# Memory attention of a two-layer perceiver: one weighting per pair laced with a memory unit's long products

## The chip, the cores and the metric

The kernel runs on one core of one Trainium2 chip. The metric is the device time of one execution in microseconds; several executions are timed and the median is taken. TensorE multiplies (the trace has its products as PE and its weight loads as PEld), VectorE is DVE, ScalarE is ACT, GpSimd is POOL, and SP issues most transfers.

## The reference, cut to what matters

Two layers of attention and feed-forward blocks work on x (32 batches of 32 tokens, 512 wide) with a context of 257 tokens per batch. The change lies in the cross attention of the second layer. The kernel's keys and values of a context token are one and the same projection (`mem`), joined to the projections of the 32 own tokens:

```python
q = split_heads(xn @ Wq)
k = split_heads(kv[..., :INNER]);  v = split_heads(kv[..., INNER:])
mem = split_heads(memories @ Wm)          # memories: 257 context tokens
k = concatenate([k, mem]);  v = concatenate([v, mem])
attn = softmax(q @ k.T * 64 ** -0.5)      # 16 heads of 64, 289 keys
out = (attn @ v) @ Wo + bo
```

## The kernel before, in words

The batches go in 16 pairs (`PAIRS`), and turn `pr` of one loop (line 1117 on, on TensorE) works on the attention of pair `pr` while it makes the memory projections of pair `pr + 1`.

**A memory unit** (`memory(pr, units)`, lines 962 to 974) is one of eight groups of 128 rows of `mem`, for both batches of a pair: twelve long products, 128 x 512 elements each, into one PSUM bank. Context and weights are split in a high and a low half so that three products of reduced precision stand for one: eight products of the context's high half (line 970; `cth`, with `wmh` and `wml` in turn over four slices k) and four of its low half (line 973, `ctl`). ScalarE makes the high half (`split_high`, line 1663) once all eight units of the pair before are done, VectorE then the low half (`split_low`, line 2407). Units 2, 3 and 4 (`BY_DVE`) use the four banks that VectorE empties, the others those of ScalarE. A bank is opened in a fixed order, and each opening waits until the one four before it was emptied.

**The weighting** (`weighted(bb)`, lines 1060 to 1089) is attention times values for one batch: three parts, block 0 and block 1 of 128 context tokens each and a tail of 33 tokens. A part is 16 small products in fp32 with a 32-column weight tile and 64 moving columns; the trace has two records for each, so 64 for the two blocks and 32 for the tail (line 1074). The three parts add up in one bank, whose filling is signalled after the tail. In the 14 middle pairs the values and probabilities come through transfers (line 2862 from `value_turn`, lines 2859 and 1752 from DRAM `probs`), which the weighting waits for.

**A turn on TensorE** (line 1117 on) issues in this order: the scores of the first batch b0 (line 1032); the weighting of the batch before, b0 - 1; units 2 and 3; the scores of b1; unit 4; units 0 and 1; the transposes of the output rows (line 1043), every fourth turn the output projection (line 1114); units 5 and 6; the tail transposes (`prob_tail`, line 1057); unit 7; the weighting of b0. Between tail transposes, then: unit 7, first weighting (b0), scores, second weighting (b0 - 1 of the next turn), units 2 and 3, scores, units 4, 0, 1, output rows, units 5, 6. `at_edge(pr)` is true for the first and the last turn, which turn their values and probabilities on TensorE instead.

**VectorE** in a turn, in program order: maxima of the first batch's scores (`maxima`, lines 2451 and 2453); the division and copy of the second weighting (`weighted`, line 2465); four 32 x 32 value transposes (`turn_values`, line 2426); copies of units 2 and 3 (line 2461); maxima of the second batch; transposes of its probabilities (line 2435); copy of unit 4; and so on to the tail copy (line 2520), `split_low`, the reciprocal (line 2528) and the division of the first weighting (line 2465 again). **ScalarE**: four exponentials for each batch as its maxima arrive (line 1689; each frees one of its banks, and the one unit 0 uses is among them), then the copies of units 0, 1, 5, 6, 7 and `split_high`. **SP**: the context of pair `pr + 2`, the next pair's own keys, value tails and queries (`load_pair`, which waits for the second weighting), the value moves, then two slices of a later stage's weights.

Of the kernel before, what the change touches and what calls it, by code (L numbers as in the profile page):

```python
# [92 lines left out]
def perceiver(nc, dram, out):  # L93
# [6 lines left out]
    with ctx:  # L100
# [3 lines left out]
        def sem(name):  # L104
            return ctx.enter_context(nc.semaphore(name))
# [5 lines left out]
        def tab(name, rows=128):  # L111
            a, n = TABLE_AT[name]
            return consts[0:rows, a:a + n]
# [49 lines left out]
        with ExitStack() as until_last:  # L163
            def shared_r(name, shape):
                return until_last.enter_context(nc.sbuf_tensor(name, shape, f32r))

            over(10240)
            ctl = shared_r("ctl", [128, 4, 2, 256])
            wmh = shared_r("wmh", [128, 2, 4, 512])
# [3 lines left out]
            wml = shared_r("wml", [128, 2, 4, 512])  # L173
# [3 lines left out]
            cth = shared_r("cth", [128, 4, 2, 256])  # L177
# [63 lines left out]
        dve_bank_full, dve_bank_free = sem("dve_bank_full"), sem("dve_bank_free")  # L241
# [113 lines left out]
        def W(name):  # L355
            return arena[:, slot_of[name], :, :]
# [40 lines left out]
        def at_edge(pr):  # L397
            return pr in (0, PAIRS - 1)
# [88 lines left out]
        def ch(c):  # L487
            return slice(512 * c, 512 * c + 512)
# [4 lines left out]
        def tl(t):  # L493
            return slice(128 * t, 128 * t + 128)
# [5 lines left out]
        def _(pe):  # L500
            stage = [0]
            mm = nc.tensor.matmul
# [7 lines left out]
            def open_act(key):  # L510
                u = UA.new(key)
                if u >= 4:
                    pe.wait_ge(act_bank_free, u - 3)
                return UA.banks[u % 4]

            def open_dve(key):
                u = UV.new(key)
                if u >= 4:
                    pe.wait_ge(dve_bank_free, u - 3)
                return UV.banks[u % 4]  # L520

            def on_act(key):
                pe.wait_ge(act_bank_free, UA.at[key] + 1)

            def on_dve(key):
                pe.wait_ge(dve_bank_free, UV.at[key] + 1)
# [57 lines left out]
            for t in range(TT):  # L584
# [4 lines left out]
                for i, (name, high, low) in enumerate((("qf", lq_high, lq_low), ("kf", lk_high, lk_low))):  # L589
                    pe.wait_ge(S["a_wlo"], i + 1)  # L590
                    b = open_dve((name, t)) if i else open_act((name, t))
# [15 lines left out]
            b = open_dve("corr")  # L607
# [7 lines left out]
            for c in range(C2):  # L615
                for k in range(4):
                    b = open_act(("agg", c, k))
                    for t in range(4 * c, 4 * c + 4):
                        last = mm(b[:, tl(t % 4)], VA[:, t, tl(k)], RA["mt"][:, t, :], start=True, stop=True)
                    last.then_inc(act_bank_full, 1)  # L620
            pe.wait_ge(S["a_wlo"], 4)
            for c in range(C2):
                on_act(("agg", c, 3))
                for o in range(4):
                    b = open_dve(("ao", o, c))
# [22 lines left out]
            for c in range(C2):  # L648
# [5 lines left out]
                b = open_act(("clock", c))  # L654
                for k in range(4):
                    last = mm(b[0:16, :], RB["cw"][:, k, :], XN[:, k, ch(c)], start=(k == 0), stop=(k == 3))
# [114 lines left out]
            for t in range(TT):  # L771
# [3 lines left out]
                b = open_act(("v", t))  # L775
                for k in range(4):
                    last = mm(b[:, :], XN[:, k, tl(t)], W("bv")[:, k, :], start=(k == 0), stop=(k == 3))
# [33 lines left out]
            for c in range(C2):  # L811
                for o in range(4):
                    b = open_dve(("bo", o, c))
                    for k in range(2 if c else 3, 4):
                        last = mm(b[:, :], W("bo")[:, k, tl(o)], RB["ot"][:, k, ch(c)], start=(k == (2 if c else 3)), stop=(k == 3))
# [44 lines left out]
            for j in range(NQ):  # L860
                for o, c in b1_order(j):
                    b = open_act(("b1", j, o, c))
# [14 lines left out]
            for c in range(C2):  # L877
# [3 lines left out]
                for k in range(4):  # L881
                    on_act(("feat", 2, c, k))
                    for i in range(4):
                        t = 4 * c + i
                        for n, (y_, w_) in enumerate(((y_high, sim_high), (y_low, sim_high), (y_high, sim_low))):
                            last = mm(four[i][:, :], y_[:, k, tl(t)], w_[:, k, :], start=(k == 0 and n == 0), stop=(k == 3 and n == 2))
                        if k == 3:
                            last.then_inc(act_bank_full, 1)
            for j in range(NQ):
                for o in range(4):  # L890
                    for c in range(C2):
                        b = open_act(("cg", j, o, c))
                        split_linear(b, ("cg", j), o, y_high, y_low, c).then_inc(act_bank_full, 1)
                        b = open_dve(("cu", j, o, c))
# [67 lines left out]
            def memory(pr, units):  # L962

                pe.wait_ge(S["d_chi"], pr + 1)
                for o in units:
# [7 lines left out]
                        last = mm(bank, wmh[:, o // 4, k, tl(o % 4)], ctl[:, k, :, :], start=False, stop=(k == 3))  # L973
                    last.then_inc(dve_bank_full if o in BY_DVE else act_bank_full, 1)

            def last_memory():

                on_act(("mrow", 1))
                b = open_act("m256")
                for o in range(OT1):  # L980
                    last = nc.tensor.transpose(b[:, 32 * o:32 * o + 32], last_rows[0:32, tl(o)], tab("ident", 32)[:, 0:32])
                last.then_inc(act_bank_full, 1)
# [32 lines left out]
            def value_blocks(bb):  # L1015

                for blk in range(2):
                    for half in range(2):
                        b = open_dve(("vt", bb, blk, half))
                        for o in range(4):  # L1020
                            last = nc.tensor.transpose(b[:, tl(o)], kts[bb // 2 % 2][:, 4 * half + o, bb % 2, 128 * blk:128 * blk + 128],
                                                       tab("ident"))
                        last.then_inc(dve_bank_full, 1)
# [33 lines left out]
                    last = nc.tensor.transpose(b[:, tl(g)], RDa["p"][:, g, 256:384], tab("ident"))  # L1057
                last.then_inc(dve_bank_full, 1)

            def weighted(bb):  # L1060

                i = bb % 2
                on_dve(("ptail", bb // 2))
                b = open_dve(("pv", bb))

                def part(lhs, rhs, first, row, stop):
                    for g in range(4):
                        for c in range(4):
                            o, par = 4 * (g // 2) + c, g % 2
                            if row is None:  # L1070
                                of = rhs[:, 2 * par:2 * par + 2, 32 * o:32 * o + 32]
                            else:
                                of = rhs[:, 128 * o + 64 * par:128 * o + 64 * par + 64].rearrange("p (a n) -> p a n", a=2)
                            last = mm(b[32 * c:32 * c + 32, 64 * g:64 * g + 64].rearrange("p (a n) -> p a n", a=2),  # L1074
                                      lhs(g, c), of,
                                      start=(first and g == 0), stop=stop, tile_position=(row or 0, 32 * c),
                                      skip_group_check=True)
                    return last

                if not at_edge(bb // 2):  # L1080
                    pe.wait_ge(values_full, 192 * (bb // 2))
                    pe.wait_ge(values_kept, 4 * (bb // 2))
                    pe.wait_ge(probs_full[i], 64 * (bb // 2))
                for blk in range(2):
                    part(lambda g, c: probs_moved[i][:, c, blk, 32 * g:32 * g + 32], RD["vt"][:, 2 * i + blk], blk == 0, None, False)
                if i == 0:
                    pe.wait_ge(tail_full[bb // 2 % 2], 32 * (bb // 4 + 1))
                part(lambda g, c: RDx["ptail"][64 * i:64 * i + 33, 0, 128 * g + 32 * c:128 * g + 32 * c + 32], RD["vtail"][64 * i:64 * i + 33, bb // 2 % 2], False, 64 * i, True
                     ).then_inc(dve_bank_full, 1)

            pe.wait_ge(S["d_wlo"], 1)
            memory(0, range(4))
# [5 lines left out]
            for h in range(2):  # L1098
                b = open_act(("mrow", h))
                for k in range(4):  # L1100
                    for i, (c_, w_) in enumerate(((last_high, wmh), (last_low, wmh), (last_high, wml))):
                        last = mm(b[0:32, :], c_[:, k, :], w_[:, h, k, :], start=(k == 0 and i == 0), stop=(k == 3 and i == 2))
# [14 lines left out]
            for pr in range(PAIRS):  # L1117
                b0, b1 = 2 * pr, 2 * pr + 1

                def fill(*units):  # L1120
                    if pr + 1 < PAIRS:
                        memory(pr + 1, [o for o in units if pr or o not in EARLY])

                on_dve(("mem", pr, 4))
                on_act(("mem", pr, OT1 - 1))
                pe.wait_ge(q_full[pr % 2], 16 * (pr // 2 + 1))
                pe.wait_ge(S["d_self"], pr + 1)
                attention_scores(b0)
                if pr:
                    weighted(b0 - 1)  # L1130
                if at_edge(pr):
                    value_blocks(b0)
                fill(2, 3)
                attention_scores(b1)
                if at_edge(pr):
                    value_blocks(b1)
                fill(4)
                fill(0, 1)
                if pr:
                    out_rows(pr - 1)  # L1140
                if pr and pr % (CB // 2) == 0:
                    on_act(("ot", pr - 1))
                    output(pr // (CB // 2) - 1)
                if at_edge(pr):
                    prob_blocks(b0)
                fill(5)
                if at_edge(pr):
                    prob_blocks(b1)
                fill(6)
                if pr == PAIRS - 1:  # L1150
                    token_rows(4, 0)
                prob_tail(pr)
                fill(7)
                weighted(b0)
# [26 lines left out]
            for c in range(C2):  # L1181
# [3 lines left out]
                b = open_act(("dl", c))  # L1185
# [4 lines left out]
            for c in range(C2):  # L1190
                b = open_dve(("bb", c))
# [3 lines left out]
            def ed_first(o, c):  # L1195
                b = open_dve(("ed", o, c))
                linear(b[:, :], e_d, tl(o), Y, ch(c), more=True)
                return b
# [10 lines left out]
            for oc in ((2, 0), (3, 0), (2, 1), (3, 1)):  # L1209
                b = ed_first(*oc)  # L1210
# [1762 lines left out]
```

## Time and profile before

| | us |
|---|---|
| median of three runs | 2051.91 (2049.27 to 2056.59) |
| the profiled execution | 2051.98 |
| its span, first to last instruction | 2050.2 |
| TensorE busy | 1970.7 (96%) |
| VectorE busy | 1237.9 (60%) |
| ScalarE busy | 874.4 (43%) |
| the loop of pairs | about 1312 to 1820 of the span |

A row of a timeline begins with its start from the span's begin and its duration, both in microseconds; then engine, line, operation, what is written and read, how many instructions are merged, and in brackets the engine's idle time before it and what ended that. "issue" means that the profile shows nothing that was waited for. The end of a product is modelled: products overlap, and a row of many is drawn until a little after the last one has made way for the next.

### The profile page before, as it was taken

What the parts mean: (1) busy time and instruction counts of PE and PEld (TensorE: products, weight loads), DVE (VectorE), ACT (ScalarE), POOL (GpSimd) and SP (SyncE); (2) the same over time, 40 slices, a digit from 0 to 9 for tenths busy, and PEclk for the clock granted to TensorE, in tenths of its full rate; (3) what the DMA queues carried; (4) which work ended last, traced back from release to release, by engine and by line L of the source; (5) the groups of instructions that cost most, each with busy time, mean ns of one, the idle gap of its engine ahead of it and who ended that gap; (6) DMA issues with size and microseconds to landing.
All of it is one profiled execution on the core that took longest, in us unless ns stands there. A gap on an engine that the chain in (4) does not pass through costs nothing. (4 is left out here: it accounts for less than half of the span.)

```text
span 2050.2 us, 34616 instructions
## 1 busy us (share of the span) xinstructions
PE 1970.7 (96%) x14134; PEld 1429.1 (70%) x14134; DVE 1237.9 (60%) x2088; ACT 874.4 (43%) x2059; POOL 118.9 (6%) x134
## 2 busy tenths in 40 slices
PE   7999999899999999999999999999999999989999
PEld 6864455578878888854445788777777777774677
DVE  6456489463355888899999511265454454548553
ACT  4224443253333333489997432233232332333342
POOL 0000000000000000110000000011101010100122
PEclk9999999999999999999999999999999999999999
DMA  7210000121110110120002235477577584743001
GB/s 269 75 58 1 1 2 3 43 98 52 41 43 21 42 62 21 62 82 21 21 1 83 65 123 148 140 202 194 149 199 197 147 215 126 201 141 98 1 0 42
DMA packets 124573, 178.93 MB, mean 87 GB/s; under 512 B 12144, under 2 KB 81264, under 8 KB 123952
## 3 DMA queue, kind: packets, MB, share of 16 engines
q1 hardware_dynamic: 114336, 162.03, 26.4%
q10 hardware_dynamic: 10080, 14.68, 2.7%
q8 instruction: 113, 1.85, 0.4%
q14 instruction: 44, 0.36, 0.1%
HBM read 124.91 MB, written 29.75 MB: 75 GB/s over the span
## 5 line engine op out<-in xcount | busy, mean ns | idle before, releaser
L1584 ACT ACTIVATE R<-R 128x64 f32<-128x64 f32 x896 | 217.0, 342 | 3.4 <-DVE R L2309 3.4
L1315 ACT ACTIVATE R<-bank 128x512 f32<-128x512 f32 (+1 forms) x134 | 79.8, 599 | 323.4 <-PE bank L973 224.4
L970 PE MATMUL bank<-cth,wmh 128*128 128x512 f32 x512 | 207.2, 405 | 5.3 <-ACT arena L1689 3.3
L970 PE MATMUL bank<-cth,wml 128*128 128x512 f32 x512 | 200.3, 391 | 0.0
L540 PE MATMUL bank<-XN,arena 128*128 128x512 f32 x320 | 147.2, 612 | 0.0
L973 PE MATMUL bank<-ctl,wmh 128*128 128x512 f32 x512 | 137.3, 390 | 0.0
L970 PEld LDWEIGHTS bank<-cth,wmh 128*128 128x128 f32 x512 | 96.1, 188 | 35.7 <-issue 14.3
L540 PE MATMUL bank<-Y,arena 128*128 128x512 f32 x256 | 116.4, 600 | 1.7 <-ACT H L1627 1.7
L1689 ACT ACTIVATE arena<-bank,small 128x289 f32<-128x289 f32 x128 | 62.9, 501 | 126.5 <-issue 125.2
L540 PEld LDWEIGHTS bank<-XN,arena 128*128 128x128 f32 x320 | 60.9, 196 | 71.1 <-issue 70.7
L973 PEld LDWEIGHTS bank<-ctl,wmh 128*128 128x128 f32 x512 | 96.1, 188 | 20.6
L970 PEld LDWEIGHTS bank<-cth,wml 128*128 128x128 f32 x512 | 96.3, 188 | 18.8 <-issue 0.5
L835 PE MATMUL bank<-hid_high,piece_high 128*128 128x512 f32 x256 | 99.8, 390 | 0.0
L835 PE MATMUL bank<-hid_high,piece_low 128*128 128x512 f32 x256 | 99.6, 389 | 0.0
L835 PE MATMUL bank<-hid_low,piece_high 128*128 128x512 f32 x256 | 99.6, 389 | 0.0
L835 PE MATMUL bank<-y_high,piece_high 128*128 128x512 f32 x256 | 99.6, 389 | 0.0
L835 PE MATMUL bank<-y_low,piece_high 128*128 128x512 f32 x256 | 99.6, 389 | 0.0
L835 PE MATMUL bank<-y_high,piece_low 128*128 128x512 f32 x256 | 99.6, 389 | 0.0
L1353 ACT ACTIVATE piece_high<-arena 128x512 fp32r<-128x512 f32 x80 | 48.8, 625 | 103.6 <-PE bank L835 102.7
L540 PEld LDWEIGHTS bank<-Y,arena 128*128 128x128 f32 x256 | 48.8, 192 | 61.4 <-issue 59.5
L540 PE MATMUL bank<-H,arena 128*128 128x512 f32 (+1 forms) x288 | 86.4, 451 | 0.0
L2520 DVE COPY XN<-bank 128x512 f32<-128x512 f32 x16 | 11.1, 691 | 117.3 <-PE bank L1057 117.3
(442 smaller groups left out, 4242.4 us busy)
## 6 DMA issues: line engine op xcount, KB each, us to landing
Y<-value_turn SPq DMA_DIRECT2D x168, 128.0 KB, 3.1
H<-in_ctxT SPq DMA_DIRECT2D x30, 512.0 KB, 5.1
arena<-in_L_attn_mlp_w SPq DMA_DIRECT2D x8, 1024.0 KB, 5.3
probs<-R SPq DMA_DIRECT2D x14, 512.0 KB, 2.9
probs<-R ACTq DMA_DIRECT2D x14, 512.0 KB, 4.9
R<-probs SPq DMA_DIRECT2D x56, 128.0 KB, 4.0
R<-probs ACTq DMA_DIRECT2D x56, 128.0 KB, 4.7
R<-value_rows SPq DMA_DIRECT2D x32, 132.0 KB
```

What stands on the lines that cost most here:

```text
L540: last = mm(bank, w[:, k, cols_], x[:, k, xc], start=(k == 0), stop=(k == 3 and not more))
L835: last = mm(b[:, :], w_, x_[:, k, ch(c)], start=(k == 0 and i == 0), stop=(k == 3 and i == 2))
L970: mm(bank, w_[:, o // 4, k, tl(o % 4)], cth[:, k, :, :], start=(k == 0 and w_ is wmh), stop=False)
L973: last = mm(bank, wmh[:, o // 4, k, tl(o % 4)], ctl[:, k, :, :], start=False, stop=(k == 3))
L1315: fn(dst, src, ACT.Copy).then_inc(act_bank_free, 1)
L1353: fn(piece_high[:, n % PIECES], W(name)[:, :, tl(o)], ACT.Copy).then_inc(S["w_high"], 1)
L1584: last = fn(into[:, x // 2, h, :, x % 2], RC["Ey"][:, t, h, :], ACT.Copy, scale=RC["Ex"][:, t, h, 8 * j + x:8 * j + x + 1])
L1689: fn(RDa["p"][:, g, 320 * (bb % 2):320 * (bb % 2) + 289], b[:, 0:289], ACT.Exp, bias=small[:, 16 + x:17 + x], scale=HD1 ** -0.5, accum_out ...
L2520: v.tensor_copy(RDx["ptail"][:, 0, :], unit(("ptail", pr))[:, :]).then_inc(dve_bank_free, 1)
```

## The change

In the 14 middle turns (1 to 14) the weighting of b0 - 1 takes unit 2 of the next pair in among its parts: four long products (k = 0 and 1) between block 0 and block 1, four (k = 2 and 3) between block 1 and the tail, and the four of the low half behind the tail. The wait for the context's high half and the opening of unit 2's bank move ahead of the weighting. Unit 3 follows as before. The first and the last turn keep the old order; in turn 0 units 2 and 3 had been made earlier, in the last turn there is nothing left to make. Nothing changes on the other engines.

```diff
+            def memory_in_parts(pr, o):
+
+                pe.wait_ge(S["d_chi"], pr + 1)
+                b = open_dve(("mem", pr, o))
+                bank = b[:, :].rearrange("p (a c) -> p a c", a=2)
+
+                def run(n):
+                    if n < 2:
+                        for k in (2 * n, 2 * n + 1):
+                            for w_ in (wmh, wml):
+                                mm(bank, w_[:, o // 4, k, tl(o % 4)], cth[:, k, :, :], start=(k == 0 and w_ is wmh), stop=False,
+                                   skip_group_check=True)
+                    else:
+                        pe.wait_ge(S["d_clo"], pr + 1)
+                        for k in range(4):
+                            last = mm(bank, wmh[:, o // 4, k, tl(o % 4)], ctl[:, k, :, :], start=False, stop=(k == 3),
+                                      skip_group_check=True)
+                        last.then_inc(dve_bank_full, 1)
+
+                return run
+
-            def weighted(bb):
+            def weighted(bb, beside=None):
 
                 i = bb % 2
                 on_dve(("ptail", bb // 2))
                 b = open_dve(("pv", bb))
+                run = (lambda n: None) if beside is None else memory_in_parts(*beside)
...
                 for blk in range(2):
                     part(lambda g, c: probs_moved[i][:, c, blk, 32 * g:32 * g + 32], RD["vt"][:, 2 * i + blk], blk == 0, None, False)
+                    run(blk)
                 if i == 0:
                     pe.wait_ge(tail_full[bb // 2 % 2], 32 * (bb // 4 + 1))
...
                      ).then_inc(dve_bank_full, 1)
+                run(2)
...
                 attention_scores(b0)
-                if pr:
-                    weighted(b0 - 1)
                 if at_edge(pr):
+                    if pr:
+                        weighted(b0 - 1)
                     value_blocks(b0)
-                fill(2, 3)
+                else:
+                    weighted(b0 - 1, (pr + 1, 2))
+                fill(3)
                 attention_scores(b1)
```

## Rows read from the trace of the kernel before

**Rows 1.** The page, queues: packets, MB, share of 16 engines.
```profile
q8 instruction: 113, 1.85, 0.4%
```
**Rows 2.** Windows of periods 2, 6, 10: length, busy of the five engines, granted clock, DMA.
```profile
1387.65:1417.63 29.98, 28.79 (x361) 22.46 (x360) 16.45 (x28) 10.70 (x27) 4.90 (x6) 1.00 0.80 204
1522.36:1552.92 30.56, 29.27 (x361) 22.66 (x360) 16.45 (x28) 10.70 (x27) 4.89 (x6) 1.00 0.80 203
1657.76:1687.71 29.95, 28.93 (x361) 22.48 (x360) 16.45 (x28) 10.70 (x27) 4.89 (x6) 1.00 0.76 201
```
**Rows 3.** The chain of waits within period 12: start, duration, what.
```profile
1743.25 4.61 DVE value_turn L2426 x4
```
**Rows 4.** Timeline of period 5 on TensorE, from the first weighting to unit 0.
```profile
1496.46 1.10 PE L1074 MATMUL bank<-Y,R 128*32 128x64 f32 x64 [0.72 <-issue]
...
1499.11 1.10 PE L1074 MATMUL bank<-Y,R 128*32 128x64 f32 x64
...
1500.14 0.65 PE L1074 MATMUL bank<-R,XN 33*32 33x64 f32 x32
...
1500.72 0.50 PE L970 MATMUL bank<-cth,wmh 128*128 128x512 f32 x1
...
1501.06 0.39 PE L970 MATMUL bank<-cth,wml 128*128 128x512 f32 x1
...
1510.89 0.47 PE L970 MATMUL bank<-cth,wmh 128*128 128x512 f32 x1 [0.30 <-ACT arena L1689]
```
**Rows 5.** Timeline of period 5 on VectorE: split, then the second weighting.
```profile
1498.21 2.29 DVE L2407 TENSOR_TENSOR ctl<-H,cth 128x2048 fp32r<-128x2048 f32 x1 [4.49 <-ACT cth L1663]
...
1502.84 0.42 DVE L2465 TENSOR_TENSOR XN<-bank,small 128x256 f32<-128x256 f32 x1
...
1503.18 4.61 DVE L2426 STREAM_TRANSPOSE value_turn<-R 128x1024 f32<-128x1024 f32 x4
```
**Rows 6.** Timeline of period 4: the last long products and the first short ones.
```profile
1464.70 1.07 PE L973 MATMUL bank<-ctl,wmh 128*128 128x512 f32 x4
1465.70 0.94 PEld L1074 LDWEIGHTS bank<-Y,R 128*32 128x32 f32 x64 [0.35 <-issue]
```
**Rows 7.** Timelines of periods 1 to 13: TensorE's idle spells around the weightings.
```profile
1361.30 1.10 PE L1074 MATMUL bank<-Y,R 128*32 128x64 f32 x64 [0.28 <-issue]
...
1364.32 1.10 PE L1074 MATMUL bank<-Y,R 128*32 128x64 f32 x64 [0.30 <-DMA R<-probs]
...
1394.85 1.10 PE L1074 MATMUL bank<-Y,R 128*32 128x64 f32 x64 [1.19 <-issue]
...
1424.51 0.70 PE L1074 MATMUL bank<-Y,R 128*32 128x64 f32 x35 [0.49 <-issue]
...
1470.84 0.30 PE L1074 MATMUL bank<-R,XN 33*32 33x64 f32 x2 [0.81 <-issue]
...
1530.24 1.10 PE L1074 MATMUL bank<-Y,R 128*32 128x64 f32 x64
...
1559.95 0.98 PE L1074 MATMUL bank<-Y,R 128*32 128x64 f32 x52 [0.69 <-issue]
...
1632.42 1.10 PE L1074 MATMUL bank<-Y,R 128*32 128x64 f32 x64 [1.38 <-issue]
...
1664.05 1.10 PE L1074 MATMUL bank<-Y,R 128*32 128x64 f32 x64 [0.30 <-DMA R<-probs]
...
1691.45 1.10 PE L1074 MATMUL bank<-Y,R 128*32 128x64 f32 x64 [0.40 <-issue]
...
1694.92 0.99 PE L1074 MATMUL bank<-Y,R 128*32 128x64 f32 x55 [0.46 <-issue]
...
1767.44 1.10 PE L1074 MATMUL bank<-Y,R 128*32 128x64 f32 x64 [1.67 <-issue]
```
**Rows 8.** DMA from 1465 to 1472 us: GB/s in 40 slices, and its instruction queue.
```profile
GB/s 0 0 0 0 0 0 0 0 0 0 0 0 0 0 0 0 0 0 94 0 0 0 0 0 0 0 0 0 0 0 0 0 0 0 0 0 0 35 129 76
...
q8 instruction: 1, 0.02, 1.3%
```

## The prediction

> **What bounds the kernel now.** I read the page first. TensorE is busy for 96% of the span, so a microsecond matters only where TensorE waits; the change touches one loop, the memory attention, which I then took apart by pair of batches. The second thing to see is queue q8, which carries instructions: 113 packets, 1.85 MB, so 16.4 KB each [rows 1]; against TensorE's 28,268 products and weight loads that is one packet for 250 of them.
>
> Second, the windows of whole periods. I number a period by the pair whose tail transposes open it; it ends at those of the next pair. Periods 2 and 10 are 29.98 and 29.95 us long, though TensorE idled for 1.19 us in one and 0.30 in the other [rows 2, 7]; period 6 is 30.56. The granted clock is 1.00, the 2.4 GHz level, in all of them. A period that ignores TensorE's idle time is set elsewhere. The chain of waits says where: it leaves TensorE for VectorE's value transposes (4.61 us) [rows 3] and returns at memory unit 0.
>
> Third, period 5 in order of time. TensorE: first weighting (of the pair's first batch) at 1496.46, scores, second weighting (of the batch before; the code's b0-1) from 1499.11, its tail part at 1500.14, long product at 1500.72, and at 1510.89 unit 0 waits 0.30 us for ScalarE [rows 4]. VectorE takes the second weighting at 1502.84, after the maxima; its four transposes, two copies and the next maxima follow it in program order, and behind those come the exponentials, which free the bank that unit 0 waits for [rows 4, 5]. So the loop goes: last unit, split of the next context, maxima, **VectorE's read of the second weighting**, transposes, maxima, exponentials, unit 0. The second weighting is ready on TensorE at 1500.79 (1500.14 + 0.65); VectorE comes 2.05 us later. That slack is what the change spends.
>
> **The change part by part.** It applies to the second weighting of 14 periods, 0 to 13.
>
> *Long products moved.* Four products go between block 0 and block 1, four between block 1 and the tail, four behind it. No arithmetic is added. Each of the two insertions ahead of the tail delays the weighting's end by: short to long 0.14 (1500.72 less the last short product, 0.22 before 1500.79, as a 64-column product is drawn 0.22 long); first to second long product 0.34 [rows 4]; two steps of 0.23 ((1.07 - 0.39) / 3 of the four-product row); and last long to first short 0.32 (1465.70 less 1464.70 + 3 x 0.227) [rows 6]; together 1.26, less the 0.04 of an unbroken step: 1.22. Two are **2.44 us**. Signalling adds 0.05, so a weighting that met no idle time is 2.49 us later, against a slack of 2.05 + 0.79 = 2.84 (period 5's 0.79 is its own idle time of 0.72 [rows 4] and the 0.07 by which a long product is drawn past the normal start). **0.35 us is to spare**; whatever TensorE idles between the first weighting and the end of the second, beyond 0.35, now goes straight into VectorE's chain. TensorE's own extra time is 2.44 - 8 x 0.227 = 0.62 us a period.
>
> *How late TensorE already is.* Idle time in front of a part pushes it by the idle figure + 0.07, inside the second weighting by about + 0.25 (the last product is drawn on) [rows 7]. Pushes: period 1, 0.28 and 0.30: 0.72. Period 3, 0.74. Period 5, 0.79. Period 7, 0.94. Period 9, 1.45. Period 10, 0.37. Period 11, 0.47 + 0.71 = 1.18. Period 13, 1.74. For 2 and 6 by starts: undisturbed, a second weighting starts 6.29 - 0.37 = 5.92 after its period (period 10: 1664.05 - 1657.76); period 2's comes at 1394.85 - 1387.65 = 7.20, a push of 1.28, period 6's at 1530.24 - 1522.36 = 7.88, a push of 1.96 [rows 2, 7]. In period 4 the 0.81 falls among the last short products, behind where long ones now stand; 8 and 12 have a smaller spell in the same place.
>
> *What becomes of the idle time.* Ahead of period 4's there is one burst of traffic, in the 19th of 40 slices of 1465 to 1472, so at 1468.2 us; those 7 us hold one instruction packet, and work goes on at 1470.84, 2.7 us after the burst [rows 7, 8]. I read the idle spells inside short products as instruction packets not yet there: the short parts issue two instructions per 16 ns product (1.03 us for 64), a packet's worth in some 2.6 us. In periods 4, 8 and 12 the long products now stand before that point, 2.44 us in which a packet can come: the spell vanishes. In 2, 3, 6, 7, 11 it comes before the first insertion and stays. The Trainium skill (Runtime: NRT & Kernel Launch, Instruction fetch mechanics) gives 16 KiB blocks, which the packet size bears out, and calls the crossing of one mostly hidden; the trace disagrees here. By the page period 4's idle time would stay and add (0.81 + 0.25) - 0.35 = 0.7 us to the sum.
>
> *The sum.* A period gets longer by its push less 0.35; but where the push is over 1.3 TensorE itself set unit 0 before (period 5: push 0.79 + wait 0.30 + 0.16 drawn over = 1.25), and only 1.3 - 0.35 = 0.95 is new. Periods 1, 2, 3, 5: 0.37 + 0.93 + 0.39 + 0.44. Periods 6, 9, 13: 3 x 0.95. Periods 7, 10, 11: 0.59 + 0.02 + 0.83. Periods 0, 4, 8, 12: nothing. Total **6.4 us**. Periods 6, 9 and 13 also lose what TensorE was later than the chain (push less 1.3: 0.66, 0.15, 0.44), time that the next period's value transfers could use; I count the last two, 0.6 us, as period 7's own spell hides the first. Against it, the second memory call may add a semaphore instruction per period, which moves the packet borders; a border that slips ahead of the waits before a first weighting would cost nothing there, and period 6's 1.96 could go, which saves 0.66 + 0.6. At even odds -0.6. Sum +6.4.
>
> *Costed at nothing.* The wait for the next context's high half, now ahead of the second weighting: ScalarE ends it at 1498.2, where period 5's VectorE split starts [rows 5], 0.9 us before the need. The low half is there 2.29 us later, at 1500.50, needed at about 1503. SP's pair load waits for the same weighting and has three short issues, then nothing until the transposes end near 1507.8: 2.4 us later it still fits, though with no more than a microsecond left. The bank opened for unit 2 was read a turn ago.
>
> *Bounds.* Switching cost below: nothing, long and short products overlap, 8 x 0.227 = 1.8 us for the weighting; the same sum then gives +1.4 us. Above: three more changes at twice 0.15 (the 0.35 of idle time on the weight load between long and short [rows 6] is the largest gap seen): 3.0 us, every period pays, +12.7 us. I take 2.44, as all its steps are rows of exactly these changes.
>
> The Trainium skill (TensorE: Matmul & The Clock Gate, Architectural detail: the array is 16x 32x32) has a 64-deep queue from which weight loads are pulled ahead of running products. The trace doesn't show it here: the load of the first short part starts with its product, 0.35 us of idle time before it [rows 6]. By the page each insertion would lose its 0.09 of switch back, and the sum would be about +5.
>
> The profiled execution took 2051.98 us (span 2050.2), the median of three 2051.91: 2051.98 + 6.4 = **2058.4 us**. About 0.3%, 6.2 us, is what a measurement tells from no change; the sum lies on that edge.
>
> **Rivals.** *Overlap:* short and long products fill each other's gaps and the slack holds. For: the short parts leave most of a 128-column array idle. Against: a gap at every change, not an overlap [rows 4, 6]. +1.4 us, 2053.4.
>
> *Faster:* TensorE paces the loop after all and the lacing feeds it instructions. All fetch spells gone: pushes of 1.28, 0.74, 1.06, 1.96, 0.94 and 0.71 are 6.7 us, 2045.3, and changes cost nothing. For: those idle spells are real. Against: periods of 29.98 and 29.95 with 1.2 and 0.3 us idle [rows 2]; no mechanism below -1.3 us while VectorE holds the loop. It decides only if unit 0 no longer waits for ScalarE in any period.
>
> *Dearer chain:* every change costs 0.3 us, and the later pair loads collide with the value transfers, which the first weighting already awaits in periods 5, 9, 13 (0.72, 1.38, 1.67 [rows 4, 7]). +12.7 us, 2064.7.
>
> **How the numbers follow.** Forecast 0.60, overlap 0.20, faster 0.07, dearer 0.13. The forecast's own spread, 4.5 to 9 us, lies above 6.2 in six of ten cases: slower 0.36 + 0.13 = 0.49; same 0.24 + 0.20 = 0.44; faster 0.07. The range, 2052.5 to 2063.5, holds the forecast's spread, most of overlap and the lower part of the dearer case. Its own range is 2056.5 to 2061.
>
> **What would show it.** In the profile after: VectorE's second-weighting row directly behind TensorE's last short product, no longer about 2 us behind it; periods of 30.3 to 30.9 us in 2, 5, 7 and 11, still 29.95 in 4 and 12; unit 0 still waiting for ScalarE, in more periods; no idle spell at the end of the second weighting. Wrong if the insertions cost under 2.0 or over 2.8 us, if VectorE still comes late to the weighting, or if periods 4 and 12 change their length.

## The result, and the profile after

The changed kernel takes 2055.87 us against 2050.53 for the one before (medians of 22 runs each): ratio 1.0027, 95% interval 1.0016 to 1.0037, so 5.3 us slower. That is small, but the interval keeps clear of 1. The forecast was 2058.4 from 2051.98, which is 6.4 us slower. The profiled execution after took 2059.92 us (span 2058.1), 4 us over its median, so its differences below add up to more than 5.3.

The chain that I expected to be hit shows it directly. VectorE's row for the second weighting, now line 2491, in period 9 (the tail transposes of this period are at 1633.18):

```profile
1644.09 0.65 PE L1096 MATMUL bank<-R,XN 33*32 33x64 f32 x32
1644.67 0.76 PEld L991 LDWEIGHTS bank<-ctl,wmh 128*128 128x128 f32 x4
1644.67 1.19 PE L991 MATMUL bank<-ctl,wmh 128*128 128x512 f32 x4
1644.81 0.42 DVE L2491 TENSOR_TENSOR XN<-bank,small 128x256 f32<-128x256 f32 x1 [1.09 <-PE bank L1096]
1645.15 4.61 DVE L2452 STREAM_TRANSPOSE value_turn<-R 128x1024 f32<-128x1024 f32 x4
```

Before, VectorE came 2.05 us after the last short product [rows 4, 5]; now it has idled for 1.09 us and starts 0.07 us after the product's drawn end (1644.74). The transposes start 11.97 us after the tail transposes, 1.19 later than the 10.78 that they have in this period before. The same in the list of waits, VectorE from 1327 to 1800 us, first the kernel before, then the changed one (columns: total us, times, longest):

```profile
DVE XN L2465 <- PE bank L1074: 3.9, 1, 3.9
```

```profile
DVE XN L2491 <- PE bank L1096: 7.5, 7, 2.9
```

The 3.9 us before are one wait at the end of the loop; its counterpart after, 3.7 us, lies just behind this stretch, at 1806 us. The seven new ones are in periods 1, 2, 6, 7, 9, 11 and 13; in 3 and 5 VectorE waits for 0.13 and 0.15 us, too little for the list.

TensorE's insertions, period 9:

```profile
1640.67 0.65 PE L1096 MATMUL bank<-Y,R 128*32 128x64 f32 x32
...
1641.25 0.50 PE L986 MATMUL bank<-cth,wmh 128*128 128x512 f32 x1
...
1641.59 0.40 PE L986 MATMUL bank<-cth,wml 128*128 128x512 f32 x1
...
1642.38 0.49 PEld L1096 LDWEIGHTS bank<-Y,R 128*32 128x32 f32 x32 [0.36 <-issue]
1642.38 0.65 PE L1096 MATMUL bank<-Y,R 128*32 128x64 f32 x32
```

One part and one insertion take 1642.38 - 1640.67 = 1.71 us, of which the part alone is 0.5 (half of the 1.03 for an unbroken 64): the 1.2 us a piece of the forecast. The first load behind the long products again starts with its product, 0.36 us idle.

Windows of whole periods (1, 2, 4, 6, 9 and 10; length, busy time of the five engines, granted clock, DMA):

```profile
1358.21:1389.11 30.90, 29.49 (x361) 22.38 (x360) 16.55 (x28) 10.81 (x27) 4.90 (x6) 1.00 0.74 197
1389.11:1422.11 33.00, 30.93 (x361) 23.27 (x360) 16.55 (x28) 10.70 (x27) 4.90 (x6) 0.95 0.71 185
1467.11:1497.09 29.98, 29.50 (x362) 22.38 (x361) 16.45 (x28) 10.70 (x27) 4.90 (x6) 1.00 0.63 173
1527.31:1557.61 30.30, 29.54 (x361) 22.41 (x360) 16.55 (x28) 10.70 (x27) 4.90 (x6) 1.00 0.75 200
1633.18:1664.33 31.15, 29.52 (x361) 22.38 (x360) 16.56 (x28) 10.71 (x27) 4.91 (x6) 1.00 0.72 198
1664.33:1694.29 29.96, 29.49 (x362) 22.39 (x361) 16.45 (x28) 10.71 (x27) 4.90 (x6) 1.00 0.73 203
```

Between tail transposes the periods changed as follows (us):

| period | forecast | measured |
|---|---|---|
| 0, 4, 8, 10, 12 | 0 | 0.0 each, within 0.04 |
| 1 | +0.37 | +0.92 |
| 2 | +0.93 | +3.02 |
| 3, 5 | +0.39, +0.44 | +0.21, +0.26 |
| 6 | +0.95 | -0.26 |
| 7, 11 | +0.59, +0.83 | +0.84, +0.65 |
| 9, 13 | +0.95 each | +1.08, +0.86 |
| sum | 6.4 | 7.6 |

Each figure is from one profile before and one after. Period 2 has an event of its own, told below. The rest of the sum is 4.6 us against a forecast of 5.5 for the same periods.

### The profile page after: what moved, and what is told of

The parts are those of the page before. It is cut to its first block and busy times, and to the rows that moved or that the text cites. A ratio compares the mean times of both kernels' runs of the same rounds, so it can differ in the third digit from the quotient of the medians.

```text
span 2058.1 us, 34630 instructions
## 1 busy us (share of the span) xinstructions
PE 1981.0 (96%) x14134; PEld 1428.4 (69%) x14134; DVE 1238.4 (60%) x2088; ACT 873.9 (42%) x2059; POOL 119.0 (6%) x134
## 5 line engine op out<-in xcount | busy, mean ns | idle before, releaser
L970 PE MATMUL bank<-cth,wmh 128*128 128x512 f32 x456 | 184.1, 404 | 5.1 <-ACT arena L1715 3.2
L970 PE MATMUL bank<-cth,wml 128*128 128x512 f32 x456 | 178.4, 391 | 0.0
L973 PE MATMUL bank<-ctl,wmh 128*128 128x512 f32 x456 | 122.3, 390 | 0.0
L970 PEld LDWEIGHTS bank<-cth,wmh 128*128 128x128 f32 x456 | 85.6, 188 | 34.3 <-issue 16.0
L973 PEld LDWEIGHTS bank<-ctl,wmh 128*128 128x128 f32 x456 | 85.6, 188 | 18.3
L970 PEld LDWEIGHTS bank<-cth,wml 128*128 128x128 f32 x456 | 85.8, 188 | 16.4
L2729 POOL COPY Y<-value_turn 32x1024 f32<-32x1024 f32 x56 | 58.0, 1036 | 403.9 <-DVE value_turn L2452 401.5
```

What stands on the lines that cost most here:

```text
L970: mm(bank, w_[:, o // 4, k, tl(o % 4)], cth[:, k, :, :], start=(k == 0 and w_ is wmh), stop=False)
L2729: g.tensor_copy(RD["vt"][part, :, a, :], value_turn[part, :, a, :]).then_inc(values_kept, 1)
```

## The experiments

Periods have the numbers of the prediction. All ratios are to the kernel before, run on the same chip beside the variant. Two theories stood against each other: that VectorE's chain, waiting for the laced weighting, takes the time; and that TensorE, with its changes between long and short products, takes it. A third question was what TensorE's idle spells inside short products are.

**VectorE divides later, in both kernels.** The division of the second weighting moves behind the four value transposes; the order in which banks are freed stays the same, and it still precedes the second maxima, whose exponentials overwrite the sums it reads.

```diff
                 maxima(b0)
-                if pr:
+                if pr and at_edge(pr):
                     weighted(b0 - 1)
...
                     turn_values(pr)
+                    weighted(b0 - 1)
                     memory(pr + 1)
```

In the changed kernel:

> The changed kernel, with VectorE's division of the second weighting moved behind the four value transposes. Theory (VectorE's chain waits for the laced weighting): the transposes begin about 10.4 us after the tail transposes in every period, however late the weighting is; periods fall back to 29.95 us where TensorE is not itself late, and some 5 us of the change's 8 us in its profile come back; about +2 to +3 us stay, from the 0.62 us of switching in the periods where TensorE is late. Rival (TensorE itself paces the loop, the switching between long and short products is the whole cost): moving a 0.4 us VectorE operation changes nothing, the kernel stays 5 to 8 us above the one before.

Measured: 2050.12 us, ratio 0.9999 (0.9988 to 1.0009), level with the kernel before. How much of that is the wait and how much the move itself, the control below tells. Period 9 of this run (1625.93 to 1656.55), the division waiting for nobody, and two windows, periods 9 and 10:

```profile
1636.48 4.62 DVE L2452 STREAM_TRANSPOSE value_turn<-R 128x1024 f32<-128x1024 f32 x4
1636.69 0.65 PE L1096 MATMUL bank<-R,XN 33*32 33x64 f32 x32
1641.03 0.39 DVE L2491 TENSOR_TENSOR XN<-bank,small 128x256 f32<-128x256 f32 x1
```

```profile
1625.93:1656.55 30.62, 29.27 (x361) 22.45 (x360) 16.24 (x28) 10.59 (x27) 4.90 (x6) 1.00 0.81 206
1656.55:1686.48 29.93, 29.47 (x361) 22.41 (x360) 16.24 (x28) 10.59 (x27) 4.90 (x6) 1.00 0.73 199
```

The transposes start before the tail part of the weighting has run, 10.55 us after the tail transposes in every one of the 13 periods from 1 to 13. TensorE issues exactly what it issued in the changed kernel, so the rival, that moving a 0.4 us operation changes nothing, is out. Periods 2, 3, 7, 9 and 13 are still 0.1 to 0.9 us longer than the quiet ones: there TensorE itself is late, by its own idle time and by the switching (period 9: 30.62).

In the kernel before, as a control:

> Control: the kernel before with the same move on VectorE. Theory: nothing waited for that weighting there (2.05 us of slack in period 5), and the chain holds the same operations in another order, so within 1 us of the kernel before. Rival (the move itself saves VectorE time, whatever the lacing): as much is gained here as by the same move in the changed kernel.

Measured: 2047.47 us, 0.9986 (0.9977 to 0.9996), so the expected nothing was wrong by 3 us. Repeated:

> The kernel before with only VectorE's division moved behind the value transposes, again: it came out 0.14% faster where I had expected nothing. If that is real (the value transposes start 0.23 us earlier after the tail, 10.55 instead of 10.78, so the values' transfers land earlier and the period is 0.05 us shorter): 0.998 to 0.9995, 1 to 4 us under the kernel before. If it was chance: 0.9995 to 1.001.

Measured: 2047.53 us, 0.9982 (0.9971 to 0.9992). The gain is real, and this is the fastest kernel of the study: 3.7 us under the one before and 8 to 9 under the changed one. Its quiet periods are 29.90 us instead of 29.95 or more, and the value transposes start 0.23 us earlier. That this earlier start, which also lets the values' transfers start earlier, is where the other 3 us come from fits the shorter wait in period 13 (1.10 us, 1.67 before), but isn't shown: that wait differs from run to run, and both profiles are of the slowest execution of their run (2052.82 and 2052.86 us).

This control also divides the loss. With the division moved in both, lacing still costs 2.65 us (2050.12 against 2047.47, on one chip); without the move it cost 5.3. So by the medians about half of the loss was VectorE's wait, and the other half stays as TensorE's lateness, as the expectation had it (+2 to +3 us). The intervals of the two ratios still overlap, so the division is good to a microsecond or two only. In the profiles, periods 0 to 13 together take 465.16 us before, 472.76 after, 465.57 in the changed kernel with the move, and 463.84 and 463.52 in the control.

**A longer chain on VectorE.** One value transpose is made twice in each of the 14 turns of the kernel before.

```diff
+                keys = kts[pr % 2][:, :, 0, 0:128].rearrange("p o (b k) -> p b o k", b=4)
+                step(v.transpose(value_turn[:, 0].rearrange("p b (o k) -> p b o k", o=8), keys))
                 for i in range(2):
                     for blk in range(2):
```

> The kernel before with the first value transpose made twice on VectorE in each of the 14 turns (1.2 us more in the chain, the same result). Theory (VectorE's chain paces the loop): every quiet period grows by about 1.25 us, 16 us in all or 0.8%. Rival (TensorE paces, with VectorE 55% busy in a period): its slack takes it, under 3 us.

Measured: 2065.78 us, 1.0068 (1.0052 to 1.0083), 14.0 us where 16 were expected. Periods 1 and 10:

```profile
1355.83:1387.07 31.24, 28.93 (x362) 22.49 (x361) 17.69 (x29) 10.70 (x27) 4.90 (x6) 1.00 0.74 195
1666.65:1697.91 31.26, 28.89 (x361) 22.46 (x360) 17.68 (x29) 10.70 (x27) 4.89 (x6) 1.00 0.71 195
```

These and all the other plain periods are 31.2 or 31.3 us long, in whatever state TensorE is: period 1 has a spell of 1.74 us and is no longer than period 10, which has none and where unit 0 waits 2.37 us for ScalarE instead. VectorE paces the loop while it is busy for 17.7 us of 31.2.

**One insertion.** Four long products between the blocks; the other eight go behind the tail.

```diff
-                    run(blk)
+                    if blk == 0:
+                        run(0)
...
                      ).then_inc(dve_bank_full, 1)
+                run(1)
                 run(2)
```

> The changed kernel with one insertion only: four long products between block 0 and block 1, the other eight behind the tail. Theory (the laced weighting reaches VectorE late): the delay is 1.25 us against 2.84 of room, so only a period whose TensorE idle time exceeds 1.6 us makes VectorE wait; the division starts 10.45 us after the tail transposes in nearly all periods, and the kernel is 1 to 2 us above the one before. Rival (each change between short and long products has its price on the path): half of the change's cost, 2.7 us or more.

Measured: 2050.62 us, 0.9992 (0.9983 to 1.0001): nothing lost, where 1 to 2 us were expected. Period 9:

```profile
1636.53 0.42 DVE L2493 TENSOR_TENSOR XN<-bank,small 128x256 f32<-128x256 f32 x1
1636.86 1.24 DVE L2454 STREAM_TRANSPOSE value_turn<-R 128x1024 f32<-128x1024 f32 x1
```

That is 10.45 us after the tail transposes, though TensorE had idled for 1.20 us; VectorE is back on its own schedule in all 14 periods. So the wait has a threshold and is not a price per insertion. TensorE's switching is still there, in periods such as 5 (30.48 us), but it comes to little: periods 0 to 13 take 466.00 us against 465.16 before.

With the division moved as well:

> One insertion of four long products, and VectorE's division behind the value transposes. Theory: VectorE's chain no longer waits for the weighting and the values start 0.2 us earlier, so this is the kernel before with the moved division (0.9986 of the one before) plus TensorE's 0.3 us of switching in the periods where it is late, less the late spells of 4, 8 and 12 that cost nothing: 0.998 to 1.000. Rival (the lacing feeds packets and pays once the chain is free): clearly under the moved division alone, 0.997 or less.

Measured: 2049.22 us, 0.9991 (0.9980 to 1.0003), as expected; lacing earns nothing once the chain is free, and is no better than the moved division alone (0.9982 beside it, 0.9986 earlier).

**Eight products ahead of an unbroken weighting.**

```diff
+                run(0)
+                run(1)
                 for blk in range(2):
                     part(...)
-                    run(blk)
```

> The changed kernel with unit 2's eight high products ahead of an unbroken second weighting, so no lacing, but nearly the same delay (about 2.0 us instead of 2.5). Theory of the delay: VectorE starts the division late by TensorE's idle time less 0.8 us. Theory of the packets: with 1.9 us of long products between the first and the second weighting, the idle spells at the start of the second weighting (periods 2, 3, 6, 7, 11 of the kernel before) vanish, since a packet has time to come; only the waits for value transfers are left, and the time is within 1 us of the kernel before. Rival (those spells are not packets but something that every start of a weighting has): they stay at 0.5 to 1.9 us, and with the delay the kernel is 2 to 4 us above the one before.

Measured: 2054.00 us, 1.0009 (0.9997 to 1.0022). VectorE's division is late in periods 2, 5, 6, 9 and 13 only, by 0.5 to 0.8 us each: 0.5 us less delay than with lacing and, by the medians, less loss, though the intervals overlap. The packet theory had put the time within 1 us of the kernel before; 2.2 us over lies on the rival's side, and is not clear of either. In 3, 7 and 11 no idle spell is left at the start of the second weighting; period 7 there runs through:

```profile
1559.93 1.10 PE L1096 MATMUL bank<-Y,R 128*32 128x64 f32 x64
1560.96 0.65 PE L1096 MATMUL bank<-R,XN 33*32 33x64 f32 x32
```

where the kernel before has 0.69 us [rows 7]. Period 2 keeps a spell of 1.18 us, but now in front of the first of the eight products, so a border that is reached before the long products is not helped by them. Period 6 has one of 1.17 in its first weighting, where values are awaited. For period 2 the packet expectation failed as I had put it.

**The borders moved.** 60 empty instructions ahead of the loop:

```diff
+            for _ in range(60):
+                pe.nop()
             for pr in range(PAIRS):
```

> The kernel before with 60 empty instructions on TensorE's queue ahead of the loop, which move every 256-instruction border 60 instructions earlier in the weightings. Theory of the packets: the same idle spells come in other periods: periods 3, 7 and 11 lose theirs, and periods 5, 9, 10 and 13 get one in the second weighting, about where 4, 8 and 12 keep theirs; the time stays within 2 us. Rival (the spells belong to the data, the banks or the transfers of those periods): the same periods keep the same spells.

Measured: 2052.11 us, 1.0001. The instruction count was still 34616 and the spells stood behind the same products: the empty instructions are not in the program that ran, and this is a repeat of the kernel before. It serves as that: 2, 3, 4, 6, 7, 8, 11 and 12 have their spells where they were (12's shows before only as a tail part drawn 1.00 us long instead of 0.65). So real ones:

```diff
                 b = open_act("m256")
+                for _ in range(30):
+                    nc.tensor.transpose(b[:, 0:32], last_rows[0:32, tl(0)], tab("ident", 32)[:, 0:32])
                 for o in range(OT1):
```

> The kernel before with 30 repeated transposes (60 instructions, the same result) on TensorE well ahead of the loop, as the empty instructions of the run before did not show in its instruction count and its spells stayed where they were. Theory of the packets: the borders lie 60 instructions earlier in every weighting: periods 3, 7 and 11 lose their spell of 0.5 to 0.9 us, period 6 loses its spell among the scores or has it late in the second weighting, and periods 5, 9, 10 and 13 get one in the second weighting; 4, 8 and 12 keep theirs or have it earlier. Time within 2 us of the kernel before. Rival: 2, 3, 4, 6, 7, 8, 11, 12 keep their spells where they were, as they did in the unmoved repeat.

Measured: 2054.88 us, 1.0035 (1.0021 to 1.0049), 34676 instructions. Period 7 without a spell, and periods 9 and 10 with new ones, late in the second weighting, where neither the kernel before nor its repeat ever had one:

```profile
1558.58 1.10 PE L1076 MATMUL bank<-Y,R 128*32 128x64 f32 x64
1559.61 0.65 PE L1076 MATMUL bank<-R,XN 33*32 33x64 f32 x32
```

```profile
1635.06 0.53 PE L1076 MATMUL bank<-R,XN 33*32 33x64 f32 x20 [0.27 <-issue]
```

```profile
1665.43 0.30 PE L1076 MATMUL bank<-R,XN 33*32 33x64 f32 x4 [0.43 <-issue]
```

3, 7 and 11 lost theirs there, 5 (0.20 us), 9, 10 and 13 got one, period 6's left the scores. The working: number TensorE's records (products, weight loads and what its sequencer ran, 28969 before) in order of start. The first record behind the spells of periods 2, 3, 4, 6, 7, 8 and 11 before is 17090, 17857, 18882, 20162, 20929, 21954 and 24001: all differences are a multiple of 256, to within 1. In the moved kernel the spells stand behind other products, but at the same remainder: 16577, 17345, 18882, 19649, 20418, 21954, 22721, 23490, 25026, 25793. And 28969 records for 113 packets are 256 a packet. That these borders stall TensorE because the next packet isn't there is the reading that fits; no run shows the packet's own wait. The spells ahead of first weightings (periods 1, 5, 9 and 13, records 16091, 19169, 22247 and 25325) are 3078 apart, not 3072, and are another thing, waits for values: before, the last transfer from `value_turn` lands at 1361.10, 1496.26, 1632.22 and 1767.24 us, each 0.20 us before the weighting starts [rows 4, 7].

The time was expected within 2 us and came out 3.7 over. The 30 transposes take 1.9 us themselves (1167.29 to 1169.18, where the original ones start), in a stage in which TensorE is busy throughout, which I had not counted, and a spell of 1.78 us now falls in period 14, where VectorE's chain doesn't cover it. That these two make up the 3.7 us is likely and not shown.

**A shorter chain.** The second maxima, too, go ahead of the two copies of units 2 and 3.

```diff
                     turn_values(pr)
-                    memory(pr + 1)
+                    weighted(b0 - 1)
                 maxima(b1)
+                if not at_edge(pr):
+                    memory(pr + 1)
```

> The kernel before with the same two moves on VectorE. Theory (VectorE's chain paces 10 of 13 periods): TensorE has 1.3 us of slack less its idle time, so each quiet period loses up to 1.2 us and a late one nothing; 5 to 7 us faster than before (about 0.3%), with less waiting of unit 0 for ScalarE, unless the value transfers become what the first weighting waits for. Rival (TensorE paces): no change.

Measured: 2052.92 us, 1.0016 (1.0004 to 1.0029): slower, a miss. Periods 8 and 13:

```profile
1594.24:1623.51 29.27, 28.97 (x361) 22.70 (x360) 16.33 (x28) 10.66 (x27) 4.90 (x6) 1.00 0.60 170
1757.95:1790.59 32.64, 30.22 (x361) 23.51 (x360) 16.69 (x28) 10.84 (x27) 4.90 (x6) 0.95 0.62 159
```

```profile
1763.71 1.31 PE L1074 MATMUL bank<-Y,R 128*32 128x64 f32 x64 [2.42 <-issue]
```

The quietest period is 0.7 us shorter, less than the "up to 1.2" expected, the other quiet ones 0.4 to 0.7, and unit 0 never waits for ScalarE. But the first weighting comes earlier and the transfers don't keep up: it idles for 1.96 us in period 5, 1.89 in 9 and 2.42 in 13, each time until 0.20 us after the last transfer from `value_turn` has landed (1492.97, 1628.55 and 1763.51), and the granted clock is 0.50 for 3.4 us behind the first and the last of these. The exception that I had named took the gain and more. This profile was taken at 2049.93 us, 3 us under the median.

> The changed kernel, the division behind the value transposes and the second maxima ahead of the copies of units 2 and 3 (two copies, 1.17 us in the chain). Theory: VectorE's chain gets 1.2 us shorter, TensorE sets unit 0 in nearly all periods, and its 0.62 us of switching now counts in all 14: 3 to 4 us below the changed kernel with the division moved alone, near the kernel before. Rival (TensorE already paces): no gain over the changed kernel.

Measured: 2057.56 us, 1.0036 (1.0017 to 1.0054), the same failure with the switching on top: idle spells of 2.15, 2.28, 2.16, 2.53 and 2.33 us in periods 1, 5, 6, 9 and 13. The rival named above, no gain over the changed kernel, has the number right, but not because TensorE's own work paces the loop: it waits.

## Why the prediction was right, point by point

- *VectorE's chain bounds the loop, with 2.05 us between the weighting and its reader.* The chain is shown by the longer one, which makes every quiet period about 1.25 us longer; the slack by the single insertion, which stays inside it and costs nothing. The division moved out of the chain brings the kernel back to the time before, but against the control with the same move half of the loss stays: once VectorE doesn't wait, TensorE's own lateness shows. The prediction has this bound (pushes over 1.3 us) and priced it for the unmoved chain only.
- *2.44 us of delay for two insertions.* An undisturbed second weighting ended 7.6 us after the tail transposes before (1335.24 less 1327.61, period 0) and ends 10.08 after (period 4): 2.5. The single insertion (1.25 us of delay, no wait) and the eight products ahead (2.0, waits of 0.4 to 0.7 us) fit the same slack of 2.84 us.
- *Quiet periods cost nothing.* 0, 4, 8, 10 and 12 are unchanged to 0.04 us, as computed.
- *The spells at the end of the second weighting vanish (4, 8, 12), those at its start stay (2, 7, 11).* So it was; period 3's is still there with 0.18 us (0.49 before). That period 4's spell of 0.81 us disappears and is worth nothing is a clear sign of what bounds this loop: TensorE gained what it was short of, in a place where it had time.
- *Period 6 at even odds.* The change has 14 instructions more, 34630 against 34616, one a period. Period 6's spell of 1.29 us among the scores is gone, and the period is 0.26 us shorter instead of 0.95 longer. I had put it at half of its worth. The 1.2 us are more than the 0.9 by which the periods other than 2 stayed under their forecast.
- *Period 2, +3.02 against +0.93.* Here a term was missing. Its spell was 1.86 us long after the change (1.19 before), and behind it the granted clock fell:

```profile
1394.00:1398.50 4.50, 2.64 (x75) 1.64 (x67) 3.54 (x5) 2.11 (x5) 0.00 (x0) 1.00 0.10 18
1398.50:1401.90 3.40, 3.40 (x44) 2.13 (x46) 1.08 (x5) 2.04 (x8) 0.00 (x0) 0.50 0.90 279
1401.90:1405.00 3.10, 3.10 (x43) 2.59 (x44) 2.45 (x3) 0.00 (x0) 0.00 (x0) 1.00 0.48 134
```

The columns are as in rows 2: 0.50, the 1.2 GHz level, for 3.4 us, after a stretch in which TensorE was busy for 2.64 of 4.50 us. Block 1 and the second insertion ran in it: the four long products and what leads to the tail took 2.00 us (1401.78 less 1399.78), 1.13 in period 9. Of the 2.1 us over the forecast, 0.7 are the longer spell and, as an estimate, the other 1.4 the clock. The kernel before has such stretches too in its repeat (below), so this is one profile's event rather than the change's, and it may explain part of the distance between the profiled 2059.92 and the median.
- *Value transfers.* Period 1's wait before the first weighting grew from 0.28 to 1.24 us, and it is also 1.02 in the unmoved repeat of the kernel before: that wait varies by a microsecond and more from run to run in periods 1, 5, 9 and 13, and so does what the lacing costs there. The sum was made from one profile. Worked out by the same rule from the spells of the repeat it is 6.9 us (an estimate), so the choice of profile was not what made it come out.
- *The signs named.* Unit 0 waits for ScalarE in 10 periods instead of 7, as forecast, and no idle spell is left at the end of a second weighting. "Periods of 30.3 to 30.9 us in 2, 5, 7 and 11" was wrong as written: 7 and 11 hold an output projection and were 44.8 us long before (45.6 and 45.4 after), period 2 took 33.0 and period 5 30.2.
- *Workings of the prediction that don't come out.* Packets of 250 instructions at two per 16 ns would last 2.0 us, not 2.6. The overlap case gives +1.5 rather than +1.4, and its upper bound of 3.0 us has four more changes, not three. None moves the forecast.
- *Where luck helped.* Period 2 was 2.1 us over its term and period 6 1.2 us under; the +0.6 for what late periods pass on to the next and the -0.6 for period 6 cancel in the sum, and no run isolates the first.

The rival *overlap* (+1.4 us) is out by the 0.36 us gaps and the 2.5 us; *faster* by the quiet periods. The sum of about +5 with weight loads that start early is nearer to 5.3 than mine, but the loads don't start early: the one in period 9 starts with its product. The *dearer chain* did not come about in the changed kernel, but its second half, first weightings that find their values not yet there, is what ended both attempts at a shorter chain. The Trainium skill (Runtime: NRT & Kernel Launch, Instruction fetch mechanics) calls the crossing of a block mostly hidden; the trace disagrees, with spells of 0.3 to 1.3 us before and up to 1.8 in its repeat, at places 256 instructions apart. The forecast of 6.4 us stands against 5.3 (3.3 to 7.6 by the interval).

## What to carry to other kernels

Before spreading a product's parts to fill an engine's gaps, look at who reads its result and what is queued behind that reader in program order: here a weighting that ended 2.5 us later, in a period in which TensorE had idled, made a 0.4 us division up to 1.2 us late (3.0 once), and with it 4.6 us of transposes and all that followed. The cheap cure is on the reader's side, to put the reading behind work that doesn't need it; that gave 0.14 to 0.18% even without the change. Give the kernel before the same cure before crediting it: here the cure hid a loss of 2.65 us that was still there. A bottleneck engine's idle spell is worth something only in the periods in which no other chain ends later, so compare the lengths of quiet and disturbed periods before counting it.

## What the runs showed of the hardware that I had not expected

- TensorE's clock can fall inside a busy loop after a single idle spell among short products: to 0.50 for 3.4 us after 1.86 us of idle time. The length of the spell alone doesn't decide it. In the shortened chain (ratio 1.0016) such stretches follow the spells of 1.96 and 2.42 us and not the one of 1.89; in its laced counterpart (1.0036) they follow 2.53 and 2.33 and not 2.15, 2.28 or 2.16. In the unmoved repeat they follow 1.77 and 1.71, and not the longer one of 1.89:

```profile
1496.99 1.10 PE L1074 MATMUL bank<-Y,R 128*32 128x64 f32 x64 [1.89 <-issue]
...
1530.09 0.67 PE L1032 MATMUL bank<-R,XN 64*32 64x289 f32 x2 [1.77 <-issue]
```

```profile
1491.75:1522.33 30.58, 28.69 (x362) 22.57 (x361) 16.46 (x28) 10.85 (x27) 4.92 (x6) 1.00 0.81 202
1522.33:1554.90 32.57, 30.80 (x361) 23.80 (x360) 17.15 (x28) 10.59 (x27) 4.91 (x6) 0.95 0.76 187
```

Periods 6 and 13 are 32.57 and 31.93 us long there, against 30.57 and 30.35 before. In the profile of the kernel before, with nothing over 1.67, there is none inside the loop's periods 0 to 14. So a spell that VectorE's chain would have covered can still cost 1 to 2 us.
- Empty instructions issued through `nop` did not arrive: same count of 34616, spells behind the same products. The number of packets says nothing here, as it is 113 with 60 real instructions more, too.
- Where the 256-instruction borders fall in bursts of short products decides over spells of 0.2 to 1.9 us each: one instruction more a turn went with the loss of period 6's, and 60 more ahead of the loop redistributed nearly all of them.
